# Reading the token pairs at tile 76 under a flag, and six of the closing adds on GpSimd

## The reference

```python
logits = jnp.einsum('bld,ed->ble', x, Wr)
probs = jax.nn.softmax(logits, axis=-1)
top_p, top_idx = jax.lax.top_k(probs, TOP_K)          # TOP_K = 2, 16 experts
gating = jnp.sum(jax.nn.one_hot(top_idx, N_EXPERTS) * top_p[..., None], axis=-2)
...
h = gelu(x @ W1e + b1e); out = h @ W2e + b2e          # one expert, 192 -> 768 -> 192
y = y + ge[..., None] * out                           # summed over the experts
...
h = h + _L0_ffn_ref(_layernorm(h), ...)               # x + y of the ffn, and the residual
```

## Time and profile before

| | us |
|---|---|
| median of 3 runs | 812.93 |
| lowest and highest of them | 812.66, 815.15 |
| the profiled execution | 818.7 |
| its span, first to last instruction | 817.0 |
| TensorE busy | 698.8 |
| VectorE busy | 459.7 |
| ScalarE busy | 373.2 |
| GpSimd busy | 387.2 |

### The profile page before, as it was taken

The page is one execution under the profiler, slowest core; times in us unless marked ns, Lnnn a source line. Parts: engine busy times, 40 slices in busy tenths (PEclk is TensorE's granted clock), DMA queues, the critical chain, the costliest instruction groups (busy, mean ns, idle before and its releaser), DMA issues.

```text
span 817.0 us, 22653 instructions
## 1 busy us (share of the span) xinstructions
PE 698.8 (86%) x7823; PEld 597.6 (73%) x7823; DVE 459.7 (56%) x1322; ACT 373.2 (46%) x892; POOL 387.2 (47%) x599
## 2 busy tenths in 40 slices
PE   0507668999999999999989989999999999999980
PEld 0407436677777777777667788999999999998980
DVE  7002124668888888888886646444444444443448
ACT  0102223666666666666656333343434454433444
POOL 7750121255777777777766534333333333333320
PEclk9999755999999999999998999999999999999995
DMA  7705462444444444444516742656527534499149
GB/s 199 134 17 84 100 188 70 110 112 98 120 109 114 109 108 109 111 111 112 122 29 186 237 107 82 189 163 189 163 77 202 150 96 114 128 259 265 50 166 327
DMA packets 96795, 110.69 MB, mean 135 GB/s; under 512 B 18625, under 2 KB 85186, under 8 KB 96386
## 3 DMA queue, kind: packets, MB, share of 16 engines
q1 hardware_dynamic: 79202, 79.56, 37.5%
q0 software_dynamic: 11792, 27.18, 10.9%
q10 hardware_dynamic: 5712, 2.79, 2.0%
HBM read 142.13 MB, written 33.96 MB: 216 GB/s over the span
## 4 chain that ended last, share of the span: by engine, by line
PE 59%; DVE 12%; issue 10%; POOL 8%; another core or an unknown queue 5%; ACT 2%; DMA 1%; SPq 1%; POOLq 1%; DVEq 0%; ACTq 0%
PE BK L491 19%; PE BK L503 19%; PE BK L825 5%; PE BK L912 4%; PE BK L953 3%; PE BK L932 2%; DVE negmax L1546 2%; POOL slot_rows L1876 2%; POOL rs L1825 2%; PE BK L964 2%; POOL hr L1865 1%; DVE hr L691 1%; PE BK L879 1%; PE BK L477 1%
## 5 line engine op out<-in xcount | busy, mean ns | idle before, releaser
L527 ACT ACTIVATE pixels<-BK,shared 128x128 f32<-128x128 f32 x474 | 130.7, 375 | 206.1 <-PE BK L491 163.4
L491 PE MATMUL BK<-pixels,shared 64*128 64x128 f32 x2844 | 174.7, 273 | 5.3 <-issue 2.6
L503 PE MATMUL BK<-shared,pixels 64*128 64x192 f32 x1896 | 175.1, 329 | 3.3 <-DVE pixels L667 2.3
L491 PEld LDWEIGHTS BK<-pixels,shared 64*128 64x128 f32 x2844 | 170.1, 188 | 7.8 <-issue 4.4
L701 POOL DMA_INDIRECT pair_rows<-pixels x79 | 77.9, 985 | 195.9 <-DVE pixels L667 191.3
L503 PEld LDWEIGHTS BK<-shared,pixels 64*128 64x128 f32 x1896 | 155.4, 189 | 6.1 <-issue 4.8
L1546 DVE TENSOR_REDUCE negmax<-BK 128x6 f32<-128x1536 f32 x64 | 112.4, 1757 | 25.4 <-PE BK L932 22.9
L1297 ACT ACTIVATE shared<-BK 128x1536 f32<-128x1536 f32 x64 | 92.7, 1448 | 10.2 <-PE BK L953 9.2
L1876 POOL DMA_INDIRECT slot_rows<-xr,adr x64 | 64.7, 1012 | 36.6 <-issue 13.6
L653 DVE TENSOR_TENSOR pixels<-pixels 128x1 int32<-128x1 f32 x64 | 10.2, 160 | 114.7 <-PE BK L477 114.7
L932 PE MATMUL BK<-shared 96*128 96x256 bf16 x384 | 56.0, 285 | 1.6 <-DMA shared<-qk_parts 0.8
(11 more groups left out here) (237 smaller groups left out, 1082.6 us busy)
## 6 DMA issues: line engine op xcount, KB each, us to landing
shared<-ew SPq DMA_DIRECT2D x158, 288.0 KB
shared<-ew SPq DMA_DIRECT2D x79, 576.0 KB
shared<-qk_parts SPq DMA_DIRECT2D x112, 96.0 KB
shared<-expert_biases SPq DMA_DIRECT2D x79, 99.0 KB
pixels<-slot_rows POOLq DMA_DIRECT2D x64, 104.0 KB
qk_parts<-shared SPq DMA_DIRECT2D x32, 192.0 KB, 2.0
shared<-qk_parts SPq DMA_DIRECT2D x16, 288.0 KB
shared<-pair_rows SPq DMA_DIRECT2D x12, 384.0 KB, 9.3
```

Source lines behind the costliest of these rows:

```text
L491: last = nc.tensor.matmul(hidden(t)[h * HC + c], w1h[w][rows, (k + h) % NK, c * P:(c + 1) * P], xtT[p][rows, k, :], start=(c == 0 and k == ...
L503: last = nc.tensor.matmul(Y[h], hT[p][rows, c * P:(c + 1) * P], w2b[w][rows, c, :], start=(c == 0), stop=(c == FC - 1))
L527: last = nc.scalar.activation(hT[p][:, c * P:(c + 1) * P], hidden(t)[c], ACT.Gelu, bias=bias[w][:, c:c + 1])
```

## The change

Three things are done.

1. **A flag.** At tile 19 VectorE writes `r_soon`: in its first column 1 if at most `SOON` = 73 tiles hold tokens, in its second the opposite.
2. **Reads at tile 76.** When SP has issued everything of the round t = 76, it loads both flags, waits until the scatters of tiles 0 to 72 have landed, and issues the reads of chunks 0 to 3 with `cond=soon`; behind the round t = 77 it issues those of chunks 4 to 7. At the end, where the reads stood, all sixteen stand again with `cond=not_soon`. So each of 16 reads is issued twice and skipped once, and both executions raise the semaphore: ScalarE and VectorE wait for 64 in place of 32.
3. **Six adds on GpSimd.** VectorE now does the multiply-adds of all eight chunks in a row. The adds of chunks 0 to 5 (`ADDED` = 6) follow on GpSimd behind its last scatter, each when `c_gated` and `c_first` have reached its chunk, and raise `c_pool`; the last two stay on VectorE, behind all multiply-adds. SP writes chunk c when `c_pool`, for the last two `c_out`, has reached it.

```diff
+    SOON = NTILE - 6
+        r_soon = late([P, 2], i32)
+        ADDED = NC - 2
@@ moe_loads (SP) @@
+            def pairs_in(chunks, when):
+                for c in chunks:
+                    for k, row in ((0, 0), (1, FIRST)):
+                        sp.dma_start(pair[k][c], pair_d[row:row + NTOK, :].rearrange("(p t) e -> p t e", t=NT)
+                                     [:, c * CT:(c + 1) * CT, :], cond=when).then_inc(s[f"ld_p{c}"], 16)
+
             for t in range(NW, NTILE):
                 ...
                 before = now
+                if t == SOON + 3:
+                    sp.wait_ge(s["r_hot"], 1)
+                    soon, not_soon = (sp.value_load(r_soon[0:1, k:k + 1], min_val=0, max_val=1) for k in range(2))
+                    for m in range(NB):
+                        sp.wait_ge(s[f"m_sc{m}"], 16 * ((SOON - m + NB - 1) // NB))
+                    pairs_in(range(0, 4), soon)
+                if t == SOON + 4:
+                    pairs_in(range(4, NC), soon)
             biases(NTILE - 1, *before)
             second(NTILE - 1, *before)
-            sp.wait_ge(s["r_hot"], 1)
             ...
+            pairs_in(range(NC), not_soon)
             for c in range(NC):
-                for k, row in ((0, 0), (1, FIRST)):
-                    sp.dma_start(pair[k][c], pair_d[...]).then_inc(s[f"ld_p{c}"], 16)
-            for c in range(NC):
-                sp.wait_ge(s["c_out"], c + 1)
+                if c < ADDED:
+                    sp.wait_ge(s["c_pool"], c + 1)
+                else:
+                    sp.wait_ge(s["c_out"], c - ADDED + 1)
@@ moe_scalar (ScalarE) and moe_vector (VectorE) @@
-                wait_ge(s[f"ld_p{c}"], 32)
+                wait_ge(s[f"ld_p{c}"], 64)
@@ moe_vector @@
+                    V.tensor_scalar(r_soon[:, 0:1], ends[:, NE - 1:NE], float(SOON - NEARLY), None, ALU.is_le)
+                    V.tensor_scalar(r_soon[:, 1:2], ends[:, NE - 1:NE], float(SOON - NEARLY), None, ALU.is_gt)
                     ...
                 last.then_inc(s["c_first"], 1)
+            for c in range(ADDED, NC):
                 h = hr[:, c * CT:(c + 1) * CT, :]
@@ moe_gpsimd @@
+            for c in range(ADDED):
+                h = hr[:, c * CT:(c + 1) * CT, :]
+                pool.wait_ge(s["c_gated"], c + 1)
+                pool.wait_ge(s["c_first"], c + 1)
+                nc.gpsimd.tensor_tensor(h, h, pair[1][c], ALU.add).then_inc(s["c_pool"], 1)
```

More of the change, by code:

```diff
@@ L318, in vit_tower @@
                  "m_x0 m_x1 m_x2 m_x3 m_wa0 m_wa1 m_wa2 m_wb0 m_wb1 m_wb2 m_f0 m_f1 m_f2 m_f3 m_tr m_xT m_s1 m_gelu m_s2 m_y "
-                 "m_sc0 m_sc1 m_sc2 m_sc3 ld_p0 ld_p1 ld_p2 ld_p3 ld_p4 ld_p5 ld_p6 ld_p7 c_first c_out c_gated "
+                 "m_sc0 m_sc1 m_sc2 m_sc3 ld_p0 ld_p1 ld_p2 ld_p3 ld_p4 ld_p5 ld_p6 ld_p7 c_first c_out c_pool c_gated "
                  "out_done dve_lane st_bias m_b0 m_b1 m_b2 r_hot").split()
@@ L442, in moe_loads @@
                 sp.wait_ge(s[f"m_sc{NB - 1 - m}"], counts[m])
+            pairs_in(range(NC), not_soon)
             for c in range(NC):
-                for k, row in ((0, 0), (1, FIRST)):
-                    sp.dma_start(pair[k][c], pair_d[row:row + NTOK, :].rearrange("(p t) e -> p t e", t=NT)
-                                 [:, c * CT:(c + 1) * CT, :]).then_inc(s[f"ld_p{c}"], 16)
-            for c in range(NC):
-                sp.wait_ge(s["c_out"], c + 1)
+                if c < ADDED:
+                    sp.wait_ge(s["c_pool"], c + 1)
+                else:
+                    sp.wait_ge(s["c_out"], c - ADDED + 1)
                 sp.dma_start(out.rearrange("b (t p) e -> p (b t) e", p=P)[:, c * CT:(c + 1) * CT, :],
@@ L539, in moe_scalar @@
             for c in range(NC):
-                act.wait_ge(s[f"ld_p{c}"], 32)
+                act.wait_ge(s[f"ld_p{c}"], 64)
                 for t in range(CT):
@@ L688, in moe_vector @@
             for c in range(NC):
-                dve.wait_ge(s[f"ld_p{c}"], 32)
+                dve.wait_ge(s[f"ld_p{c}"], 64)
                 for t in range(c * CT, (c + 1) * CT):
```

## The result

The changed kernel is slower. Its median is 822.35 us (4 runs, 820.3 to 823.85) against 812.79 us for the kernel before (4 runs, 812.41 to 815.15): a ratio of 1.0103, with a 95% interval of 1.0068 to 1.0138. Two later measurements, on two chips and with more runs, gave 1.0065 (1.0032 to 1.0098) and 1.0060 (1.0034 to 1.0085), so the loss is nearer to 5 us than to the 9.6 us of the first.

A forecast was written before the change was run, and what follows sets the result against it. TensorE was taken to set the pace up to 794.1 us, then VectorE; adds +3.6, SP's queue +2.5 and clock +1.7 sum to +7.8 us, so 820.7 us (chance 0.48), range 814.5 to 826.

The forecast's parts named there:

- What bounds the end: Last stretch: from 794.79 us VectorE sets the pace, 2.38 us a round, and waits for no transfer.
- The parts at no cost: Two comparisons at tile 19, under 0.4 us, and sixteen skipped reads at the end, 6.7 us, all hidden.
- GpSimd's add: One 128x768 add on GpSimd at the end takes 1.83 us, against VectorE's 0.96.
- VectorE is held meanwhile: At the end, VectorE's multiply-adds with two SBUF inputs stand until GpSimd's add is done.
- Its price: At the end, six adds cost 6 x (1.83 - 0.15) = 10.1 us; with VectorE's savings, net +3.6 us.
- SP's queue: Early reads ahead of tile 78's first weights in SP's queue delay its up-projection: +2.5 us.
- x: SP's time for one conditional early read: 0.64 to 0.73 us, taken as 0.68; bounds 0.48 and 0.88.
- The formula: Tile 78's first weights are issued at 778.3 us plus sixteen conditional read times, 789.2 us.
- The clock: After TensorE stands about 2.3 us before tile 78, 3.4 us of matmuls run at half speed: +1.7 us.
- rival 1: TensorE's stop before tile 78 costs no clock: +6.1 us, 819.0 us; chance 0.20.
- Rival 3: GpSimd and VectorE don't shut each other out at the end: 810.9 us with SP's stop (0.08), 806.7 without (0.06).
- rival 2: SP is in time for tile 78, so only the adds count: +3.6 us, 816.5 us; chance 0.18.

The follow-up runs named there:

- reads alone: Kernel before plus only the flag and early reads, all eight adds left on VectorE: ratio 1.0009; first multiply-add of the end to span end 22.17 us.
- the kernel with the late second group: Kernel before plus flag and early reads, adds on VectorE, second eight reads issued behind tile 78's last issue and not ahead of its first: ratio 1.0013.

## Why the prediction was right or wrong

- **What bounds the end: right.** VectorE never waited for a read there. With the reads up to 14 us earlier (reads alone) B is 22.17 us in place of 22.19.
- **The parts at no cost: right.** The two comparisons take 0.30 us together. The sixteen skipped reads stand 0.33 us apart, not 0.42, from 790.47 to 795.5. ScalarE's first gating starts at 790.95, 0.04 us behind its last gelu, and the profile shows no wait in front of it.
- **GpSimd's add: right.** 1.83 us from two rows, 1.84 measured.
- **VectorE is held meanwhile: right, and shown.** The multiply-add with two SBUF inputs is held, the one with a PSUM addend isn't, and the loss goes with the add's length.
- **Its price: the term of 1.68 us an add was mis-sized.** It is 1.53 us (19.90 - 10.7, divided by six). The step that failed is the 0.15 us hidden. The row has more: VectorE lost 0.73 us of an add of 1.00, so 0.27 us were hidden. The prediction left out the 0.12 us before VectorE's instruction came, but in a stream of them another one runs in that time, and the measured 0.3 us are what the row gives. The saving was mis-sized a little too: VectorE's own work falls to 10.7 + 1.8 = 12.5 us and not 12.7. VectorE's end grew by 2.5 us, less than the lower bound of 2.8, and 0.4 us came behind the last add, which the sum didn't have: 2.9 in place of 3.6. GpSimd's adds went in ahead of queued multiply-adds six times of six, but it isn't always VectorE that waits: in the changed kernel with a PSUM addend, GpSimd's last add lost 1.7 us beside VectorE's adds.
- **SP's queue: right in kind and place, x mis-sized.** A conditional read costs 0.585 us, with 0.25 in front and 0.33 for the transfer, and not 0.68; L445's 0.36 to 0.45 were lengths of reads issued back to back. The formula with the right x gives 0.9 us, and 1.6 were measured. Tile 78's two skipped issues took 0.86 us and not 0.54, tile 76's two small ones 0.6 and not 0.4, and 0.15 us are left. Why the first pair took longer isn't shown: it took 0.54 in the kernel with the late second group, while in the one with all sixteen reads at tile 76 the pair right behind them took 0.55 and the next one 0.86. The forecast was 2.5.
- **The clock: this step failed.** I took a fall for likely after a stop of 2.3 us, from one row with a stop of 1.84. The stops were 1.33, 1.58 and 1.44 us in the three traces of the changed kernel, and the clock stayed at 1.00; the term was nothing and rival 1 had the mechanism. That a longer stop does lower it, and for about the price I gave, is shown by the kernel with all sixteen reads at tile 76: 3.45 us idle, then 1.6 us lost in one block. What a stop between 1.6 and 3.4 us does at this place, the forecast 2.3 among them, no run shows. The upper bound of +3.1 was wrong as well: 6.2 us of matmuls, all at half speed, would cost 6.2.
- **The sum.** +7.8 us was forecast, the traces have +4.5 to +4.8, and the medians of three measurements +9.6, +5.6 and +4.2. The terms were too large by two thirds. That the predicted 820.7 us lies so near the first median, 822.35, is luck: by the traces' +4.5 to +4.8, the same base gives 817.4 to 817.7. The sign, the range and the two mechanisms were right. Rival 3 is refuted; rival 2's condition, SP in time, is what the kernel with the late second group fulfils, and there A is as before.

What stays open is why the first measurement's interval (1.0068 to 1.0138) leaves out the 1.0055 to 1.0065 that the traces and the later runs give. No trace shows a further loss, and the later measurements agree with each other; that four executions of each kernel were too few for this spread is likely, and not shown.

## What to carry to other kernels

An add moved from VectorE to GpSimd did not run beside VectorE's work here but in its place, since both add instructions read SBUF and VectorE's had a second SBUF input. Before moving anything, look at how long VectorE's instructions last while GpSimd computes; with the addend in PSUM none of 32 was held. A transfer that is issued earlier costs its issue in the queue, here 0.6 us each and 0.33 if it is skipped, in front of all that stands behind it; count up to the next one that somebody waits for. And early data is worth something only with work that uses it early: with three chunks' reads and work put into VectorE's idle time ahead of the end, the kernel became 0.8% faster.

## What the runs showed of the hardware

A read whose address is formed from a register and which may be skipped costs SP 0.585 us against 0.47 to 0.49 for a plain one (nine in a row start within 4.37 us in the kernel before), although the transfer instruction itself is shorter, 0.33 us; a skipped one costs 0.33 us. Single issues of such reads took 1.23 and 1.38 us, without a cause that the runs show. Both directions of the holding occur: VectorE by 1.55 us for an add of 1.84, GpSimd by 1.7 us beside VectorE's two of 0.95. An idle time of TensorE of 1.25 to 1.58 us left the granted clock at 1.00 behind it, one of 3.45 us, and the one of 1.84 us in the earlier trace rows, were followed by windows at 0.57 and 0.50. And one binary on one chip spread from 809.2 to 819.6 us over 31 executions. Where their difference lies is seen only in the traced ones: the stretches A and B repeated to 0.1 us in the kernels that leave tile 78's start alone, so in these it lies ahead of the last 63 us.
